# Graph attention on one core: GpSimd waits for a step's four gathers before it issues the next four

## The chip, the cores and the metric

The kernel runs on one core of a Trainium2 chip. The metric is the device time of one execution, in microseconds. The kernel before took 6796.57 us, the median of three runs (6765.51 to 6805.92).

## The reference, cut to what matters

The program has eight layers on a graph of 3125 nodes and 50000 edges, each node with 256 features. Layers 0, 2, 4 and 6 work on the graph, the others are mixtures of experts. The change lies in the third graph layer alone, which is attention over the edges, run twice (two inner layers of weights):

```python
def _ga_layer(h, src, dst, Wq, Wk, Wv, Wo, g, b):
    q = (h @ Wq).reshape(n, H, DK)          # 8 heads of 32
    k = (h @ Wk).reshape(n, H, DK)
    v = (h @ Wv).reshape(n, H, DV)
    e = jnp.sum(q[dst] * k[src], axis=-1) / np.sqrt(DK)
    m = jax.ops.segment_max(e, dst, num_segments=n)
    a = jnp.exp(e - m[dst])
    z = jax.ops.segment_sum(a, dst, num_segments=n)
    alpha = a / (z[dst] + 1e-09)
    msg = v[src] * alpha[:, :, None]
    agg = jax.ops.segment_sum(msg, dst, num_segments=n).reshape(n, H * DV)
    return _layer_norm(agg @ Wo + h, g, b)
```

For each edge the row of its source node is needed: its keys and its values, 2 times 256 floats. These rows lie side by side in a table in HBM, and a gather fetches them.

## The kernel before, in words

The edges are sorted by their destination and cut into 416 chunks of 128 edges (CHUNKS). A gather fetches the 128 rows of one chunk, 2 KB each, from the table `pairs` to the 128 partitions; it is an indirect DMA that GpSimd issues, with a column of `by_dst_idx` as its list of rows. Four chunks (GS) are a step, so an attention has S = 104 steps and 416 gathers, and the two of them have 832.

A step's rows go to one of ten slots (SLOTS): seven in the tile `held`, three more lent by the tile `xn`, whose content is parked in HBM meanwhile. Each slot has a semaphore of its own, `gathered[j]`, which rises by 16 with each gather that lands. GpSimd's part is the loop below. Before step i it waits until VectorE has done the messages of step i - 10 (`weighed`), whose slot it will fill.

```python
for i in range(S):
    if i == HELD:
        pool.wait_ge(parked, 16)
    if i >= SLOTS:
        pool.wait_ge(weighed, i - SLOTS + 1)
    for n in range(GS):
        k = GS * i + n
        nc.gpsimd.indirect_dma_start(rows(i)[:, n, :], None, K.pairs, ...).then_inc(gathered[i % SLOTS], 16)
```

The other engines run through loops of S + 9 steps written out in full, each with its own order. In VectorE's step i stand, in this order:

- `multiply(i - 2)`, line 1954: two products of queries (in PSUM) and keys (gathered). It is the one place that waits for `gathered`.
- in some steps `shift`, `lower` or `rescale`, lines 2004 to 2027, for the running maximum of the softmax. Every four steps (GW) make a wave of 128 rows of scores, and these parts stand once in a wave.
- `place(i + 1)`, line 1850: the one-hot matrices of the next step.
- `peaks_of_rows` once in a wave, lines 1981 to 1984.
- `score(i - 2)`, line 1963: the sums over the features of a head.
- `weigh(i - 8)`, line 1971: the values times their weights; it gives the slot back to GpSimd.
- `carry` once in a wave, lines 1992 to 2000.

So the gathers of step i may begin after VectorE's step i - 2, and their rows are wanted in its step i + 2.

TensorE makes the queries of the edges (line 2071) from transposed one-hots (line 2126), and sums the messages by node (line 2085). ScalarE copies the transposed one-hots out of PSUM (line 2184) and the sums of finished nodes to the result (lines 2159, 2161). SyncE only parks `xn` and fetches it back after the last step that uses the lent slots. There are other indirect DMAs in the kernel (lines 387, 1608, 1614), in other stages; no change touches them.

Of the kernel before, what the change touches and what calls it, by code (L numbers as in the profile page):

```python
# [57 lines left out]
GS = 4  # L58
# [1800 lines left out]
SLOTS = HELD + LENT  # L1859


def attention(nc, K, edges, G, q, acc):
# [6 lines left out]
    with stage(nc) as st:  # L1869
# [20 lines left out]
        gathered = [st.sem(f"gathered{j}") for j in range(SLOTS)]  # L1890
# [12 lines left out]
        def rows(i):  # L1903
            j = i % SLOTS
            return held[:, j, :, :] if j < HELD else lent[:, j - HELD, :, :]
# [5 lines left out]
        def load(engine, where, most):  # L1911
            _, values = nc.values_load_multi_w_load_instructions(
                where, [engine], min_val=0, max_val=most,
                skip_runtime_bounds_check_because="number_chunks writes tiles that there are and starts of banks of sums")
            return values

        with nc.Block() as block:

            @block.gpsimd
            def _(pool):  # L1920
                for i in range(S):
                    if i == HELD:
                        pool.wait_ge(parked, 16)
                    if i >= SLOTS:
                        pool.wait_ge(weighed, i - SLOTS + 1)
                    for n in range(GS):
                        k = GS * i + n
                        nc.gpsimd.indirect_dma_start(rows(i)[:, n, :], None, K.pairs,  # L1928
                                                     bass.IndirectOffsetOnAxis(ap=edges.idx[:, k:k + 1], axis=0))\
                            .then_inc(gathered[i % SLOTS], 16)  # L1930
# [780 lines left out]
```

## Time and profile before

| | |
|---|---|
| median of the runs | 6796.57 us |
| lowest and highest | 6765.51 and 6805.92 us |
| profiled execution: its own time | 6830.38 us |
| profiled execution: span from first to last instruction | 6828.6 us |
| GpSimd (POOL) busy | 2167.3 us, 32% of the span |
| first gather of the first attention, last start of a gather | 2976.6 us, 3732.2 us |
| first gather of the second attention, last start of a gather | 3947.7 us, 4723.4 us |

Every duration and point of time further down is of the profiled execution, which took 33.8 us more than the median of the runs. POOL is GpSimd, DVE is VectorE, ACT is ScalarE, PE is TensorE's matmuls. In an engine's timeline the columns are start, duration, engine, line, operation and tiles; in brackets stand the idle time before the instruction and what ended it. A gather's duration there is the time that GpSimd is busy with issuing it, not the time until its rows have landed.

### The profile page before, as it was taken

To read this page: it belongs to the slowest core of one execution; us is meant where nothing else is said; L and a number is where in the kernel's file an instruction comes from. 1 tells how busy PE (TensorE), PEld (TensorE's weight loads), DVE (VectorE), ACT (ScalarE), POOL (GpSimd) and SP (SyncE) were. 2 spreads that over 40 slices of the span, in tenths; PEclk is the share of its full clock that TensorE was granted. 3 is DMA by queue.
4 is the path that set the end of the run, shared out by engine and by line. 5 is a ranking of instruction groups with operands and counts; after the bars stand their busy time and mean duration, and the time that the engine had idled before them with its cause. 6 is when DMAs were issued, how large, how long until landed. Compare 5 with 4: busy or idle time off the path is not lost. (4 is left out here: it accounts for less than half of the span.)

```text
span 6828.6 us, 83598 instructions
## 1 busy us (share of the span) xinstructions
PE 4909.0 (72%) x21926; PEld 3369.3 (49%) x21975; DVE 2801.8 (41%) x6736; ACT 1757.8 (26%) x4567; POOL 2167.3 (32%) x2105
## 2 busy tenths in 40 slices
PE   2521649998794979567777657777679599999944
PEld 2410327745691458445555435555578544444443
DVE  4271459901324032447767456666332302020242
ACT  1220115400220012125555325555232200000020
POOL 3356220054345514236655055554004200000024
PEclk9999999999797978789889788888788799999966
DMA  0000003254464415445544154544115532424233
GB/s 15 1 1 1 1 26 135 99 187 135 134 196 139 145 56 184 152 134 149 150 134 133 55 156 133 142 138 123 55 44 180 178 138 74 177 73 174 77 89 113
DMA packets 345481, 755.43 MB, mean 111 GB/s; under 512 B 106057, under 2 KB 179380, under 8 KB 342006
## 3 DMA queue, kind: packets, MB, share of 16 engines
q1 hardware_dynamic: 185702, 435.52, 18.6%
q0 software_dynamic: 114208, 281.05, 14.6%
q10 hardware_dynamic: 45296, 35.56, 1.7%
q8 instruction: 129, 2.11, 0.1%
q14 instruction: 146, 1.20, 0.1%
HBM read 634.70 MB, written 117.24 MB: 110 GB/s over the span
## 5 line engine op out<-in xcount | busy, mean ns | idle before, releaser
L1178 PE MATMUL banks<-ring,xn 128*128 128x512 f32 (+1 forms) x3500 | 1349.0, 548 | 121.3 <-PEq L126 104.6
L1178 PEld LDWEIGHTS banks<-ring,xn 128*128 128x128 f32 x3500 | 627.9, 191 | 843.0 <-issue 826.0
L1928 POOL DMA_INDIRECT held<-pairs,by_dst_idx x592 | 644.5, 1089 | 829.4 <-POOLq L126 379.7
L2071 PE MATMUL banks<-agg,hotT 128*128 x1664 | 519.9, 442 | 226.3 <-ACT hotT L2184 119.0
L387 POOL DMA_INDIRECT dst_table<-nodes_pay,nodes_row x392 | 387.9, 990 | 777.1 <-DVEq L1152 404.7
L387 POOL DMA_INDIRECT bin_table<-bins_pay,bins_row x392 | 403.6, 1030 | 591.7 <-ACTq L795 205.3
L2071 PEld LDWEIGHTS banks<-agg,hotT 128*128 128x128 f32 x1664 | 328.7, 214 | 339.4 <-issue 291.6
L2159 ACT ACTIVATE x<-banks x832 | 323.5, 389 | 601.6 <-PE banks L2085 357.8
L1652 PE MATMUL banks<-second,hT 128*128 x1544 | 390.1, 392 | 41.0 <-ACT hT L1670 15.8
L1637 PE MATMUL banks<-xT,w1r 128*128 128x128 f32 x3088 | 402.5, 283 | 21.0 <-DVE xT L1690 8.7
L1670 ACT ACTIVATE hT<-banks,b1T 128x128 f32<-128x128 f32 x772 | 224.5, 368 | 721.6 <-PE banks L1637 528.9
L2085 PE MATMUL banks<-bins_pay,hot 128*128 128x264 f32 x832 | 290.3, 460 | 159.9 <-issue 110.8
L1637 PEld LDWEIGHTS banks<-xT,w1r 128*128 128x128 f32 x3088 | 381.6, 199 | 24.9 <-issue 18.1
L1070 PE MATMUL banks<-spans,lanes 128*128 128x256 f32 x1440 | 332.0, 387 | 77.6 <-DVE spans L1051 65.4
L1189 ACT ACTIVATE agg<-banks 128x512 f32<-128x512 f32 (+1 forms) x70 | 34.8, 549 | 1348.3 <-PE banks L1178 1348.3
L2509 DVE TENSOR_SCALAR yT<-banks,columns 128x512 f32<-128x512 f32 (+1 forms) x42 | 27.2, 689 | 839.5 <-PE banks L2490 839.5
L1698 DVE TENSOR_TENSOR bins_pay<-banks,bias 128x256 f32<-128x256 f32 x235 | 99.8, 425 | 646.8 <-PE banks L1652 537.8
L1556 POOL MEMSET second<- 64x8192 f32 x1 | 6.9, 6919 | 1126.5 <-POOLq L126 1126.5
L725 PE MATMUL banks<-places,loT 64*128 64x14 bf16 (+1 forms) x784 | 177.4, 226 | 241.8 <-issue 127.3
L2085 PE MATMUL banks<-nodes_pay,hot 128*128 128x264 f32 x832 | 279.7, 434 | 95.5 <-issue 69.9
L1614 POOL DMA_INDIRECT home_rows<-bins_pay,home x235 | 233.1, 992 | 360.8 <-DVE bins_pay L1698 343.8
L1070 PEld LDWEIGHTS banks<-spans,lanes 128*128 128x128 f32 x1440 | 266.5, 191 | 144.0 <-issue 111.2
(382 smaller groups left out, 8158.3 us busy)
## 6 DMA issues: line engine op xcount, KB each, us to landing
ring<-adjacency SPq DMA_DIRECT2D x145, 1280.0 KB
w1r<-in_L_ffn_W SPq DMA_DIRECT2D x114, 512.0 KB
adjacency<-strips SPq DMA_DIRECT2D x13, 3200.0 KB
w1r<-in_L_ffn_w SPq DMA_DIRECT2D x65, 512.0 KB
rows<-home_rows SPq DMA_DIRECT2D x35, 640.0 KB
ring<-adjacency SPq DMA_DIRECT2D x25, 640.0 KB
table<-xn SPq DMA_DIRECT2D x100, 128.0 KB
pairs<-ring SPq DMA_DIRECT2D x50, 256.0 KB
```

The lines of the kernel that those rows point to most:

```text
L387: self.nc.gpsimd.indirect_dma_start(self.table, bass.IndirectOffsetOnAxis(ap=self.row[:, c:c + 1], axis=0), self.pay[:, c * W:(c + 1) * W] ...
L725: nc.tensor.matmul(bank, loT[h * L:(h + 1) * L, c % 4, b * P:(b + 1) * P], places[h * L:(h + 1) * L, c * UB + b, :, :].rearrange("p d n -> ...
L1070: nc.tensor.matmul(K.banks[:, bass.ds((v % 16) * SPAN_S, SPAN_S)], lanes[:, j, q, :], spans[:, j, q, :], start=False, stop=True, skip_grou ...
L1178: last = nc.tensor.matmul(K.ps[2 * (g % 2) + o][:, 0:wd], x[:, t * D + o * P:t * D + (o + 1) * P], ring.buffer[:, n % R, 0:wd // cols, q * ...
L1614: nc.gpsimd.indirect_dma_start(K.home_rows, bass.IndirectOffsetOnAxis(ap=r.home[:, c:c + 1], axis=0), yr[:, c % R, :], None).then_inc(stor ...
L1637: last = nc.tensor.matmul(K.ps[2 + jj % 2][:, h * P:(h + 1) * P], w1r[:, jj, s, h * P:(h + 1) * P], xT[:, jj % 2, s * P:(s + 1) * P], star ...
L1652: last = nc.tensor.matmul(bank, hT[:, jj % 2, h * P:(h + 1) * P], ahead.second[:, bass.ds(e * (nh * D) + h * D, D)], start=(h == 0), stop= ...
L1670: last = nc.scalar.activation(hT[:, j % 2, h * P:(h + 1) * P], K.ps[2 + j % 2][:, h * P:(h + 1) * P], func, bias=b1T[:, bass.ds(e * nh + h ...
L1928: nc.gpsimd.indirect_dma_start(rows(i)[:, n, :], None, K.pairs, bass.IndirectOffsetOnAxis(ap=edges.idx[:, k:k + 1], axis=0))\
L2071: last = nc.tensor.matmul(queries(c, part)[:, n % 2 * D:(n % 2 + 1) * D], hotT[:, c % 2, n * P:(n + 1) * P], tile_of(q, at[n]), start=True ...
L2085: nc.tensor.matmul(K.banks[:, bass.ds(starts[n], W)], hot[:, g % HOTS, n, :], K.spare[g % MSGS][:, n * W:(n + 1) * W], start=False, stop=T ...
L2159: nc.scalar.activation(tile_of(acc, t, W), bank, ACT.Copy).then_inc(kept, 1)
```

## The change

One wait is added to GpSimd's loop. Before it issues the four gathers of step i, it waits until the four of step i - 1 have landed. Nothing is removed or moved, and the number of gathers, their order and their slots stay as they were.

```diff
                     if i >= SLOTS:
                         pool.wait_ge(weighed, i - SLOTS + 1)
+                    if i:
+                        pool.wait_ge(gathered[(i - 1) % SLOTS], 16 * GS * ((i - 1) // SLOTS + 1))
                     for n in range(GS):
                         k = GS * i + n
                         nc.gpsimd.indirect_dma_start(rows(i)[:, n, :], None, K.pairs,
```

## Rows read from the trace of the kernel before

**Rows 1.** The page: the span, and the gathers' group of instructions.

```profile
span 6828.6 us, 83598 instructions
...
L1928 POOL DMA_INDIRECT held<-pairs,by_dst_idx x592 | 644.5, 1089 | 829.4 <-POOLq L126 379.7
```

**Rows 2.** The two attentions in windows from VectorE's first product to its last.

```profile
core 0: us, PE busy (x) PEld busy (x) DVE busy (x) ACT busy (x) POOL busy (x), PEclk, DMA share, GB/s
...
2991.93:3746.20 754.27, 540.57 (x2198) 382.18 (x2196) 515.21 (x938) 381.62 (x1037) 438.06 (x410) 0.87 0.51 144
...
3963.12:4737.36 774.24, 545.51 (x2196) 383.99 (x2194) 515.06 (x939) 381.44 (x1037) 433.52 (x410) 0.86 0.50 140
```

**Rows 3.** Line 1928, both attentions: what ended GpSimd's idle time (us, times), and who waited.

```profile
L1928 POOL DMA_INDIRECT held<-pairs,by_dst_idx x592: 947/953/7122, 2976.6 to 4723.4; - x198
...
  DVE nodes_pay L1971: 289.5, 41
...
  DVE bins_pay L1971: 103.5, 27
...
  DVE held L1954: 19.2, 6
```

**Rows 4.** GpSimd's timeline, start of each attention: fourth gathers of a step, and the fortieth.

```profile
2988.10 0.95 POOL L1928 DMA_INDIRECT held<-pairs,by_dst_idx  x1 [0.30 <-issue]
...
2998.15 0.95 POOL L1928 DMA_INDIRECT held<-pairs,by_dst_idx  x1 [0.30 <-issue]
...
3033.63 0.96 POOL L1928 DMA_INDIRECT xn<-pairs,by_dst_idx  x1 [0.30 <-issue]
...
3959.20 0.95 POOL L1928 DMA_INDIRECT held<-pairs,by_dst_idx  x1 [0.30 <-issue]
```

**Rows 5.** VectorE's timeline: products that waited for those gathers, and the last ones.

```profile
2991.93 1.29 DVE L1954 TENSOR_TENSOR held<-banks,held 128x512 f32<-128x512 f32 x2 [5.64 <-DMA held<-pairs,by_dst_idx]
...
3001.82 1.29 DVE L1954 TENSOR_TENSOR held<-banks,held 128x512 f32<-128x512 f32 x2 [1.75 <-DMA held<-pairs,by_dst_idx]
...
3746.20 1.28 DVE L1954 TENSOR_TENSOR held<-banks,held 128x512 f32<-128x512 f32 x2
...
3963.12 1.29 DVE L1954 TENSOR_TENSOR held<-banks,held 128x512 f32<-128x512 f32 x2 [5.71 <-DMA held<-pairs,by_dst_idx]
...
4737.36 1.28 DVE L1954 TENSOR_TENSOR held<-banks,held 128x512 f32<-128x512 f32 x2
```

**Rows 6.** GpSimd's timeline: four gathers after a wait for VectorE's messages.

```profile
3221.44 0.95 POOL L1928 DMA_INDIRECT held<-pairs,by_dst_idx  x1 [3.19 <-DVE nodes_pay L1971]
3222.69 1.17 POOL L1928 DMA_INDIRECT held<-pairs,by_dst_idx  x1 [0.30 <-issue]
3224.17 1.96 POOL L1928 DMA_INDIRECT held<-pairs,by_dst_idx  x1 [0.30 <-issue]
3226.43 0.95 POOL L1928 DMA_INDIRECT held<-pairs,by_dst_idx  x1 [0.30 <-issue]
```

**Rows 7.** VectorE's timeline of the same stretch.

```profile
3219.96 1.22 DVE L1971 TENSOR_TENSOR nodes_pay<-held,weights 128x1024 f32<-128x1024 f32 x1
3221.09 1.28 DVE L1954 TENSOR_TENSOR held<-banks,held 128x512 f32<-128x512 f32 x2
...
3222.36 0.68 DVE L1850 TENSOR_TENSOR hot<-iota,by_dst_pay 128x512 f32<-128x512 f32 x1
...
3224.09 1.21 DVE L1971 TENSOR_TENSOR bins_pay<-held,weights 128x1024 f32<-128x1024 f32 x1
3225.22 1.28 DVE L1954 TENSOR_TENSOR held<-banks,held 128x512 f32<-128x512 f32 x2
```

**Rows 8.** Windows after the last gather of a burst has been issued (columns as in rows 2).

```profile
3385.46:3387.55 2.09, 2.09 (x13) 1.49 (x11) 0.82 (x4) 1.25 (x4) 0.00 (x0) 1.00 0.67 214
3387.75:3392.50 4.75, 2.20 (x8) 1.63 (x9) 4.68 (x9) 2.58 (x8) 0.63 (x1) 0.87 0.00 0
```

**Rows 9.** ScalarE's and GpSimd's timelines, around the end of the first forty gathers.

```profile
3032.68 0.60 ACT L2184 ACTIVATE hotT<-banks 128x512 f32<-128x512 f32 x1 [25.42 <-remote]
```

```profile
3056.24 0.95 POOL L1928 DMA_INDIRECT held<-pairs,by_dst_idx  x1 [21.65 <-DVE bins_pay L1971]
```

**Rows 10.** VectorE's timeline, two products one step apart.

```profile
3400.82 1.28 DVE L1954 TENSOR_TENSOR held<-banks,held 128x512 f32<-128x512 f32 x2
...
3412.98 1.27 DVE L1954 TENSOR_TENSOR xn<-banks,xn 128x512 f32<-128x512 f32 x2
```

## The prediction, made before the change was run

> **What bounds the kernel now.** I read the page first, for the size of the matter: 592 of the 832 gathers stand in one group there, 1089 ns each [rows 1]. Then windows over the two attentions: from the first product to the last they take 754.27 us and 774.24 us, and no engine fills them; TensorE is busy for 540.57 of the 754.27 us, VectorE for 515.21, GpSimd for 438.06, the DMA engines for half [rows 2]. An attention has 104 steps, so 103 intervals lie between its first and last product: 7.32 us and 7.52 us a step. Then the line of the gathers: GpSimd's idle time is ended 68 times by VectorE's line 1971, 393.0 us in all (289.5 + 103.5), while VectorE waited for gathered rows six times, 19.2 us [rows 3]. All six lie in the first steps. So the gathers run ahead and the computing engines set the pace, in a ring of dependences between TensorE, ScalarE and VectorE. The reader is to see that GpSimd has slack, about 190 us in each attention, and that the question is whether the added wait is larger.
>
> **The change: one wait, 103 times in each attention.** What it makes is a loop of GpSimd and the DMA engines alone: issue four, wait for the landing of the fourth, issue four. Behind the wait on GpSimd's queue stand only gathers; SyncE's and the other queues are not touched. Who waits for the gathers is VectorE's line 1954. The length of the loop is a sum of four terms.
>
> (1) From the first issue to the fourth: three intervals of 0.95 us issue and 0.30 us gap [rows 4], 1.256 us each, 3.77 us.
>
> (2) From the start of the fourth issue to the moment its rows can be used. The trace shows it where VectorE waited for it: the fourth gather began at 2988.10 and the product at 2991.93, 3.83 us; the twelfth at 2998.15 and the product at 3001.82, 3.67 us; in the second attention 3959.20 and 3963.12, 3.92 us [rows 4, 5]. I take 3.8 us. Those gathers had others right behind them, which the new loop won't have. The other end: after the last issue of a burst ended, at 3385.46, data flowed for 2.09 us more and then the DMA engines stood still [rows 8]; with 0.95 us of issue that is 3.0 us, and the semaphore can't come earlier. So 3.0 to 3.9.
>
> (3) GpSimd's start after a semaphore. After line 1971 ended at 3221.18 (3219.96 + 1.22), GpSimd began at 3221.44, 0.26 us later, and VectorE's product began with the same event or a little before [rows 6, 7]. In term 2 VectorE's start is already contained, so I add 0.2 us; the ends are 0.1 and 0.35.
>
> (4) Stretched issues. An issue takes 0.953 us at the median and 1.089 us in the mean [rows 1, 3]: 0.136 us by four, 0.54 us a step. The timelines show where it comes from. The third gather after 3221.44 began at 3224.17 and took 1.96 us, while VectorE's line 1971 ran from 3224.09 to 3225.30; the second began at 3222.69, inside line 1850 (3222.36 to 3223.04), and took 1.17 us [rows 6, 7]. Line 1954 does not do this. In this example the four span 4.99 us instead of 3.77. In the new loop GpSimd and VectorE are released by the same event, the landing, so they stand to each other as in these rows, in which both were released together: about 1.3 us in two of a wave's four steps (plain ones, with line 1971 some 3 us after the product), and 0.1 to 0.4 us in the two where the maximum's work delays line 1971. That mean would be 0.8 us. I take 0.7, between this and 0.54.
>
> The rule behind term 4 is in the Trainium skill, "SBUF — State Buffer", section "Who interferes with whom": a VectorE instruction with two SBUF inputs contends with a GpSimd instruction that reads SBUF, and the later one blocks. The trace agrees (line 1971 and line 1850 have two SBUF inputs, line 1954 has one in PSUM). The same section infers that such an instruction doesn't hinder the making of descriptors; the 1.96 us issue speaks against this for indirect gathers, which read their indices. By that inference term 4 would be nothing, and the loop 0.7 us shorter.
>
> The loop: 3.77 + 3.8 + 0.2 + 0.7 = 8.47 us a step.
>
> **What hides it.** The computing engines need 7.32 and 7.52 us a step in the mean, less than the loop. They do need more in single steps (12.2 us between two products, 3400.82 and 3412.98 [rows 10]), but the gathers of step i may begin four steps before they are wanted, and that lead carries such a step. So the loop sets the pace nearly everywhere. The first rows land as before, at 2991.9 and 3963.1. The last product then comes 103 times 8.47 = 872.4 us after the first: 118.2 us later than now in the first attention (872.4 - 754.27), 98.2 us in the second. The work after the last product is the same. Sum: +216 us.
>
> A second way to count it: each wait costs GpSimd 3.8 + 0.2 less the 0.95 us of issue and the 0.30 us gap that were there, 2.75 us, by 103 is 283 us. By 2 it is 566 us, of which 393 us of idle time [rows 3] can swallow at most that much: +173 us, and +206 with 0.16 us more stretch a step. The two agree.
>
> Profiled, 6830.4 + 216 = 7046 us; the profiled execution was 33.8 us above the median, so for the median 6796.6 + 216 = **7013 us**, 3.2% slower.
>
> **Something that speaks for the change.** During the first forty gathers, which run without a pause to 3033.63 [rows 4], ScalarE stood for 25.42 us before a copy at 3032.68, put down to nothing local, although TensorE's transposes had their last recorded end long before; when the burst was over this stopped. GpSimd then idled 21.65 us until 3056.24 [rows 9]. If a long burst holds back other engines, spacing the gathers removes that, and the computing engines alone could be quicker than 7.3 us. With a loop of 8.47 us it doesn't matter how much quicker: the gain is only in how the first ten steps run, and the sum from first to last product contains it. It would matter if the loop were shorter.
>
> **Rivals.**
> *The landing is quick enough, and nothing changes.* The loop would have to be 7.1 to 7.75 us (206 intervals times p, less 1528.5 us, within 68 us of zero; 68 us, 1%, is about what a measurement of this kernel can tell from no change). With term 2 at 3.0, term 3 at 0.1 and term 4 at 0.54 it is 7.41, so -2 us: 6795 us. For it: the drain of 2.09 us [rows 8]. Against it: three measured waits of 3.67 to 3.92 [rows 4, 5]. 12%.
> A sentence apart: by the Trainium skill, "DMA: Bandwidth & Descriptors", section "Anatomy of one DMA — SWDGE (gpsimd) path", a DMA takes 2.0 us plus its bytes by 436 GB/s, 2.6 us for 256 KB as an estimate from that page. Counted from the start of the issue this would give the same rival, with a loop of some 7.3 us; counted from its end it gives 3.55 us and the forecast. The rows above lie with the second.
>
> *Faster.* The burst is what holds TensorE's results back, in later bursts too, and the loop is short. Were it 6.9 us, the time would fall by 107 us, to 6690 us. It decides from a loop below 7.1 us, for which the landing has to come 2.5 us after the fourth issue begins, less than the 3.0 us at which data still flowed [rows 8]. 3%.
>
> *Slower than forecast: both bounds add up.* Two ways to the same price. The slow single steps outlast the lead, so that VectorE gives the slot back late and the loop starts late; or TensorE, which waits longer in each step, is granted less of its clock than the 0.87 of now [rows 2] and needs its 5.2 us a step (540.57 by 104) nearly twice. Either gives about 9.2 us a step: +367 us, 7164 us. For it: rows 10. Against it: 12.2 us is one step among four. 18%.
>
> *The wait does nothing.* It would have to be over when GpSimd comes to it. That holds where GpSimd idles longer than 2.75 us for line 1971 anyway; there are at most 68 such places [rows 3] for 206 waits, and they are in the second count above. No chance of its own.
>
> **How the numbers follow.** Forecast (loop 7.9 to 8.9 us) 67%, unchanged 12%, faster 3%, both bounds 18%. The range leaves out the faster case and most of the unchanged one, and takes in the upper one but for its tail: a loop of 7.65 us gives 6796.6 + 47 = 6844, of 9.2 us 7164; 6850 to 7165 us. Faster by over 1% 3%, within 1% 12%, slower by over 1% 85%.
>
> **What the new profile would show.** Right, if GpSimd's idle time before line 1928 is ended by the landing of gathers some 200 times with nearly 3 us each; if VectorE's line 1954 waits for the gathers in most steps; if groups of four gathers start about 8.5 us apart, with the third often 1.9 us long; if the two windows from first to last product are near 872 us. The burst of forty is gone, and ScalarE's 25 us wait with it. Wrong, if the landing comes 3 us after the fourth issue starts, or if VectorE still never waits for rows.

## The result, and the profile after

The changed kernel took 7101.47 us, the median of three runs (7095.71 to 7102.41), against 6796.57 us before: 1.0434 times as long, 95% interval 1.0399 to 1.0469. The profiled execution took 7095.71 us; against the profiled one of before that is 265 us more, between the medians it is 305 us. The profiled execution of before lay 34 us above its median, that of after 6 us below its own.

The page of the changed kernel, its span and the gathers' group (line 1930 is line 1928 of before):

```profile
span 7094.0 us, 83788 instructions
...
L1930 POOL DMA_INDIRECT held<-pairs,by_dst_idx x592 | 665.3, 1124 | 998.5 <-DMA held<-pairs,by_dst_idx 423.4
```

The two windows from VectorE's first product to its last, as in [rows 2]:

```profile
2987.98:3885.36 897.38, 593.95 (x2196) 416.98 (x2194) 515.60 (x938) 384.36 (x1042) 447.41 (x412) 0.84 0.44 121
4101.70:5004.23 902.53, 603.79 (x2194) 421.43 (x2194) 515.10 (x939) 383.72 (x1042) 452.03 (x412) 0.82 0.43 120
```

The reader is to see that the work in them is the same as before, VectorE's 515 us within half a microsecond, while the windows have grown by 143.1 us (897.38 - 754.27) and 128.3 us (902.53 - 774.24). That is 271.4 us, all of the 265.4 us between the spans and a little more. By 103 intervals the steps take 8.71 and 8.76 us, where they took 7.32 and 7.52.

Line 1930 of the changed kernel: what ended GpSimd's idle time, and who waited for gathers (compare [rows 3]):

```profile
  DMA held<-pairs,by_dst_idx: 489.5, 144
...
  DMA xn<-pairs,by_dst_idx: 203.2, 60
...
  DVE held L1956: 548.0, 148
...
  DVE xn L1956: 217.3, 60
```

GpSimd now waits for landings 204 times, 3.4 us each, and no longer for VectorE's messages at all. VectorE waits for gathered rows at each of its 208 pairs of products. Both stand still for the same event, which is what a loop of issue and landing looks like from its two sides.

GpSimd's timeline over one step and the start of the next:

```profile
3173.78 0.95 POOL L1930 DMA_INDIRECT held<-pairs,by_dst_idx  x1 [3.37 <-DMA held<-pairs,by_dst_idx]
3175.04 0.96 POOL L1930 DMA_INDIRECT held<-pairs,by_dst_idx  x1 [0.30 <-issue]
3176.30 1.86 POOL L1930 DMA_INDIRECT held<-pairs,by_dst_idx  x1 [0.30 <-issue]
3178.47 0.96 POOL L1930 DMA_INDIRECT held<-pairs,by_dst_idx  x1 [0.30 <-issue]
3182.81 0.95 POOL L1930 DMA_INDIRECT held<-pairs,by_dst_idx  x1 [3.39 <-DMA held<-pairs,by_dst_idx]
```

VectorE's timeline beside it:

```profile
3173.11 1.29 DVE L1956 TENSOR_TENSOR held<-banks,held 128x512 f32<-128x512 f32 x2 [1.93 <-DMA held<-pairs,by_dst_idx]
...
3176.12 1.22 DVE L1973 TENSOR_TENSOR bins_pay<-held,weights 128x1024 f32<-128x1024 f32 x1
3182.14 1.29 DVE L1956 TENSOR_TENSOR held<-banks,held 128x512 f32<-128x512 f32 x2 [4.80 <-DMA held<-pairs,by_dst_idx]
```

From these the terms can be read for one step. The fourth issue began at 3178.47 and the product that needs it at 3182.14: 3.67 us. GpSimd, released by the same landing, began at 3182.81: another 0.67 us. The four issues span 4.69 us, 0.92 more than 3.77, with the third stretched while line 1973 (1971 of before) ran beside it.

### The profile page after: what moved, and what is told of

It reads as the page before. It is cut to its first block and busy times, and to the rows that moved or that the text cites. A ratio compares the mean times of both kernels' runs of the same rounds, so it can differ in the third digit from the quotient of the medians.

```text
span 7094.0 us, 83788 instructions
## 1 busy us (share of the span) xinstructions
PE 5023.2 (71%) x21926; PEld 3443.5 (49%) x21975; DVE 2802.3 (40%) x6736; ACT 1761.6 (25%) x4567; POOL 2192.3 (31%) x2105
## 5 line engine op out<-in xcount | busy, mean ns | idle before, releaser
L1930 POOL DMA_INDIRECT held<-pairs,by_dst_idx x592 | 665.3, 1124 | 998.5 <-DMA held<-pairs,by_dst_idx 423.4
L2073 PE MATMUL banks<-agg,hotT 128*128 x1664 | 553.2, 463 | 254.9 <-DVE held L1956 151.2
L2087 PE MATMUL banks<-bins_pay,hot 128*128 128x264 f32 x832 | 349.2, 538 | 308.3 <-DVE banks L2029 256.4
L1956 DVE TENSOR_TENSOR held<-banks,held 128x512 f32<-128x512 f32 x296 | 190.8, 686 | 548.0 <-DMA held<-pairs,by_dst_idx 548.0
L2087 PEld LDWEIGHTS banks<-bins_pay,hot 128*128 128x128 f32 x832 | 205.8, 272 | 382.7 <-issue 351.4
```

The lines of the kernel that those rows point to most:

```text
L1956: V.tensor_tensor(keys, queries(c, hh)[:, 0:2 * D].rearrange("p (c d) -> p c d", d=D), keys, ALU.mult).then_inc(product if hh else halved, 1)
L2073: last = nc.tensor.matmul(queries(c, part)[:, n % 2 * D:(n % 2 + 1) * D], hotT[:, c % 2, n * P:(n + 1) * P], tile_of(q, at[n]), start=True ...
L2087: nc.tensor.matmul(K.banks[:, bass.ds(starts[n], W)], hot[:, g % HOTS, n, :], K.spare[g % MSGS][:, n * W:(n + 1) * W], start=False, stop=T ...
```

## The experiments

They ran in three groups, each on one chip, beside the kernel before on that chip. The kernel before took 6719 us on the chip of the first group, 6109 us on that of the second and 6112 us on that of the third, a third chip. Within a chip its runs differ by less than 1%. So ratios are compared within a group, and steps across groups. A trace of the kernel before exists for the chip of the result ("the first chip" below) and for that of the third group; for the first and second groups only its times are known. The changed kernel itself ran on the first chip and in the third group.

**Waiting for fewer of the four.** Three runs in which GpSimd waits for the first three, two or one gathers of the step before. For these the waited-for gathers have semaphores of their own, and VectorE waits for both:

```diff
+        EARLY = 3    # 2 in the second run, 1 in the third
+        early = [st.sem(f"early{j}") for j in range(SLOTS)]
...
-                        pool.wait_ge(gathered[(i - 1) % SLOTS], 16 * GS * ((i - 1) // SLOTS + 1))
+                        pool.wait_ge(early[(i - 1) % SLOTS], 16 * EARLY * ((i - 1) // SLOTS + 1))
...
-                            .then_inc(gathered[i % SLOTS], 16)
+                            .then_inc((early if n < EARLY else gathered)[i % SLOTS], 16)
```

> GpSimd waits only for the first three gathers of the step before (they have a semaphore of their own; VectorE waits for both). Theory, the loop of issue and landing sets the pace: the loop loses one issue interval of 1.26 us, from the 8.74 us of the changed kernel to about 7.4 us a step; the 2 times 103 intervals then take about as long as in the kernel before, 6800 us in all, within 40. Rival, the added wait costs something else than the loop (waits that add up with the computing engines' own slow steps): the steps stay near 8.2 us or more, 6960 us or more.

Measured: 6777.94 us, 1.0092 times the kernel before (1.0075 to 1.0109); 7.25 us a step. The step lost 1.5 us for one issue left out of the loop, where 1.26 us were expected, and the rival's 8.2 us or more did not come. GpSimd's idle time is ended by landings 177 times here, by VectorE's messages 28 times, so the loop still sets most steps, but not all. Windows from the first product to the last of the first attention, waiting for three:

```profile
2981.23:3728.10 746.87, 548.97 (x2196) 386.54 (x2194) 517.15 (x938) 381.30 (x1042) 439.53 (x411) 0.89 0.51 146
```

> GpSimd waits only for the first two gathers of the step before. The loop is about 6.2 us, shorter than the 7.3 to 7.5 us a step of the kernel before, so the loop can't slow it. Theory of the bursts (long runs of gathers without a pause hold TensorE's results back, and the loop allows at most four gathers in 6.2 us): the steps come down to 6.2 to 6.8 us, 150 to 250 us less than the kernel before, 6550 to 6650 us. Rival (the pace of the kernel before is that of its computing engines and has nothing to do with bursts): 6800 us, within 30.

Measured: 6649.29 us, 0.9907 (0.9882 to 0.9931): 0.9% faster than the kernel before on that chip, 70 us, about half of the 150 us that the theory of the bursts gave at least. The steps came to 6.56 and 6.63 us. Waiting for two, the same window:

```profile
2986.25:3662.29 676.04, 513.45 (x2198) 364.43 (x2196) 513.79 (x939) 380.02 (x1037) 445.79 (x410) 0.92 0.57 161
```

> GpSimd waits only for the first gather of the step before. The loop is then no longer than the four issues, about 5.0 us, so bursts are nearly what they were. Theory of the bursts: little or nothing is gained, 6750 to 6800 us. Rival: 6800 us as well; together with the run that waits for two it shows whether the pacing or the wait itself matters.

Measured: 6722.76 us, 1.0011 (0.9996 to 1.0025), 6.96 us a step. So the wait as such does nothing, and what helps on that chip is the pace of two, although GpSimd has to wait for a landing only 40 times with it, 30.7 us in all (29 times and 8.9 us when it waits for one).

The traces of these slower chips also say what the pace does to the late results of TensorE that the prediction describes under "Something that speaks for the change". They appear as waits of ScalarE and VectorE that are put down to nothing on the core ("remote"). Summed over the two attentions they come, on the chip of this group, to 268 us with a wait that never holds GpSimd up (the next run), 297 us waiting for one gather, 196 us waiting for two, and none at all waiting for three. On the first chip they come to 417 us in the kernel before and to none in the changed kernel. For ScalarE's copy of the transposes alone, the kernel before (line 2184) and the run that waits for one (line 2189) have:

```profile
  remote: 122.5, 36
```

```profile
  remote: 66.0, 13
```

So long bursts and late results go together on these chips. But where the pace is slow enough that none is left, the loop is itself about as long as the steps were with them, 7.25 us waiting for three.

**The wait without its content.** It stands where it stood, for gathers long landed:

```diff
-                    if i:
-                        pool.wait_ge(gathered[(i - 1) % SLOTS], 16 * GS * ((i - 1) // SLOTS + 1))
+                    if i >= 3:
+                        pool.wait_ge(gathered[(i - 3) % SLOTS], 16 * GS * ((i - 3) // SLOTS + 1))
```

> The wait stands where it stood, but for the step three before, whose gathers have landed by then. What is left is the instruction. Theory: as the kernel before, 6800 us within 30, since GpSimd has some 190 us of slack in each attention and the instruction costs at most 0.5 us a step. Rival, the wait as an instruction is what costs: 6900 us or more.

Measured: 6716.89 us, 1.0003 (0.9986 to 1.0021). Its line 1930 shows the idle time before gathers ended by VectorE's messages again and not by landings, as in [rows 3]:

```profile
  DVE nodes_pay L1973: 174.2, 33
  DVE bins_pay L1973: 109.8, 30
  DMA xn<-pairs,by_dst_idx: 0.3, 1
```

The instruction is free while GpSimd has slack; the cost of the change is the landing. One detail matters below. Here too two waits stand in front of the first gather of a step, and the one that comes true last is VectorE's. GpSimd and VectorE's line 1973:

```profile
3122.93 0.95 POOL L1930 DMA_INDIRECT held<-pairs,by_dst_idx  x1 [3.37 <-DVE bins_pay L1973]
```

```profile
3121.43 1.23 DVE L1973 TENSOR_TENSOR bins_pay<-held,weights 128x1024 f32<-128x1024 f32 x1 [4.74 <-ACT weights L2179]
```

GpSimd starts 0.27 us after the end of line 1973 (3121.43 + 1.23), and it does so all 63 times, exactly as in the kernel before with its single wait (68 times, 0.27 us).

**Only one wait in front of a gather.** The wait for VectorE's messages is moved one gather ahead:

```diff
-                    if i >= SLOTS:
-                        pool.wait_ge(weighed, i - SLOTS + 1)
...
                     for n in range(GS):
                         k = GS * i + n
+                        if n == GS - 1 and SLOTS <= i + 1 < S:
+                            pool.wait_ge(weighed, i + 1 - SLOTS + 1)
```

> The changed kernel, but the wait for VectorE's messages moves from the first gather of a step to the last gather of the step before, so that no gather has two waits in front of it. Theory, term 3 of the sum was too small (0.2 us) because the second wait becomes an instruction of its own, after which GpSimd starts 0.67 us behind VectorE's product instead of 0.17: the loop loses 0.5 us in some 93 steps of each attention, 8.74 to about 8.25 us, and the time against the kernel before falls from 1.043 to about 1.030. Rival, the start is slow for another reason (VectorE holding the port, the landing seen later by GpSimd): 8.7 us and 1.043 stay.

Measured: 8.22 and 8.25 us a step, as expected. 6604.63 us, 1.081 (1.0792 to 1.0828), not 1.030: the expected ratio went by the kernel before of the first chip, and on this chip that kernel is 10% faster. The changed kernel was not run on this chip. The nearest comparison is with the third group, where the kernel before takes the same time within 0.1%: the changed kernel has 1.0988 and 8.70 and 8.74 us a step there. GpSimd's timeline in this run:

```profile
2805.91 0.95 POOL L1930 DMA_INDIRECT held<-pairs,by_dst_idx  x1 [3.06 <-DMA held<-pairs,by_dst_idx]
...
2815.04 0.95 POOL L1930 DMA_INDIRECT held<-pairs,by_dst_idx  x1 [3.00 <-DMA held<-pairs,by_dst_idx]
```

And VectorE's:

```profile
2805.74 1.29 DVE L1956 TENSOR_TENSOR held<-banks,held 128x512 f32<-128x512 f32 x2 [1.74 <-DMA held<-pairs,by_dst_idx]
...
2814.88 1.29 DVE L1956 TENSOR_TENSOR held<-banks,held 128x512 f32<-128x512 f32 x2 [4.91 <-DMA held<-pairs,by_dst_idx]
```

GpSimd now begins 0.17 us after VectorE's product instead of 0.67, and the rival falls. The changed kernel's own trace shows the same thing within a few steps: up to step 9 of an attention only the new wait stands in front of the first gather (but for step 7, which waits for `parked` as well), from step 10 on both. The first gathers of steps 9 and 10 on GpSimd, and VectorE's products released by the same landings:

```profile
3053.29 0.95 POOL L1930 DMA_INDIRECT xn<-pairs,by_dst_idx  x1 [2.84 <-DMA xn<-pairs,by_dst_idx]
...
3062.11 0.95 POOL L1930 DMA_INDIRECT held<-pairs,by_dst_idx  x1 [3.13 <-DMA xn<-pairs,by_dst_idx]
```

```profile
3053.12 1.29 DVE L1956 TENSOR_TENSOR xn<-banks,xn 128x512 f32<-128x512 f32 x2 [4.77 <-DMA xn<-pairs,by_dst_idx]
...
3061.43 1.29 DVE L1956 TENSOR_TENSOR xn<-banks,xn 128x512 f32<-128x512 f32 x2 [2.37 <-DMA xn<-pairs,by_dst_idx]
```

0.17 us, then 0.68. (Step 7, at 3036.62, starts 0.70 us after its product.) The page of the changed kernel also counts 190 instructions more than that of the kernel before (83788 and 83598), and this run only 2 more. So a second wait beside the wait for the landing costs 0.5 us. A second wait as such does not: in the run for the step three before it stood there as well, and the start came at the usual 0.27 us. Which property decides, the order of the two or what the last one waits for, is open; the two waits in the other order were not run.

**VectorE's work, with and without its second SBUF input.** Both kernels leave out as much of VectorE's time (the windows show 438.08 and 435.49 us where it was 515); one takes it from the weighing, which reads two tiles in SBUF, the other from the sums, which read one.

```diff
-                    V.tensor_tensor(msg[g % MSGS][:, :, 0:DH]..., rows(g)[:, :, D:2 * D]..., ALU.mult)
+                    V.tensor_tensor(msg[g % MSGS][:, 0:HEADS, 0:DH]..., rows(g)[:, 0:1, D:2 * D]..., ALU.mult)
```

> The changed kernel with VectorE's weighing of the messages (two inputs in SBUF) done for one of the four chunks of a step; the other three quarters of this work are left out. Theory, term 4: this instruction stretches issues by up to 1 us, and the loop shortens by 0.4 to 0.7 us a step, from 8.74 to 8.0 to 8.3 us. If the loop didn't set the pace but VectorE's work did, it would shorten by the 0.9 us that are left out.

Measured: 8.41 and 8.45 us a step, 0.29 less than with all the work (8.70 and 8.74, third group). The direction is that of term 4, the size smaller than expected: issues take 404.86 by 412 = 0.983 us in the window below instead of 447.85 by 412 = 1.087, 0.42 us less a step, of which 0.29 arrive. The traces say where the rest stays. In the first attention the time from the first to the fourth issue's start falls from 4.23 to 3.94 us, all of the 0.29; the other 0.12 us are the fourth issue's own length, and from its start to the product it takes 3.84 us with the full work and 3.85 with a quarter.

```profile
2632.49:3499.21 866.72, 601.47 (x2198) 423.26 (x2196) 438.08 (x939) 383.70 (x1042) 404.86 (x412) 0.82 0.45 125
```

```diff
-                    V.tensor_reduce(scores[:, v % 2, at:at + GS * HEADS]..., rows(c)[:, :, 0:D]..., AX.X, ALU.add)
+                    V.tensor_reduce(scores[:, v % 2, at:at + HEADS]..., rows(c)[:, 0:1, 0:D]..., AX.X, ALU.add)
```

(the scores of the other chunks are set to zero once).

> The changed kernel with VectorE's sums over the features (one input in SBUF) done for one of the four chunks of a step; three quarters of this work are left out, as much VectorE time as in the run before. Theory, this instruction doesn't hold up an issue, and its absence only shifts the weighing by 0.9 us: the loop stays at 8.4 to 9.0 us. If VectorE's work set the pace, 7.8 us.

Measured: 8.67 and 8.68 us a step, 0.03 and 0.06 less than with all the work:

```profile
2631.42:3524.64 893.22, 600.32 (x2198) 422.85 (x2196) 435.49 (x938) 382.90 (x1042) 443.09 (x412) 0.83 0.44 122
```

So as much VectorE time as in the run before is taken away and next to nothing arrives. VectorE's work is behind the loop, and what matters of it is when it keeps GpSimd from issuing.

**Three gathers in the first ten steps, two afterwards.**

```diff
-                        pool.wait_ge(early[(i - 1) % SLOTS], 16 * EARLY * ((i - 1) // SLOTS + 1))
+                        pool.wait_ge(early[(i - 1) % SLOTS], 16 * (2 * ((i - 1) // SLOTS) + 3))
...
-                            .then_inc((early if n < EARLY else gathered)[i % SLOTS], 16)
+                            .then_inc((early if n < (3 if i < SLOTS else 2) else gathered)[i % SLOTS], 16)
```

> GpSimd waits for three gathers of the step before in the first ten steps and for two afterwards. Theory of the bursts: the stall of some 35 us in the steps 3 to 5, which the run that waits for two still has, goes, and each attention gains 10 to 15 us over it; 0.986 to 0.988 of the kernel before, against 0.991. Rival, the stall at the start comes from something else than the burst of forty gathers: 0.991.

Measured: 6169.88 us, 1.0095 (1.0079 to 1.0112), a loss. On this chip the kernel before was itself 10% faster than on the first, and this run's trace has no late results in the attentions, so it says nothing on the stall at the start.

**The same kernels on one more chip.** Nothing was edited.

> The kernel before once more, for its profile on this chip. On the chip of the second group of runs it took 6109 us, where the first trace was of an execution of 6830 us. Theory: the DMA engines and each single instruction take the same time on all chips, and what differs is TensorE's late results while gathers flow; so where the whole time is near 6110 us, the steps of the attention are near 5.9 us and no copy of ScalarE waits 10 us or more for a transpose that has ended; where it is near 6750 us, the steps are 6.9 to 7.5 us and such waits are there. Rival: the chip's instructions or its memory are faster throughout.

Measured: 6110.53 us. The windows of the kernel before on this chip:

```profile
2631.65:3231.34 599.69, 489.78 (x2198) 346.45 (x2196) 511.70 (x939) 377.53 (x1037) 465.94 (x410) 0.98 0.66 181
3447.14:4047.22 600.08, 487.76 (x2194) 344.78 (x2194) 512.60 (x938) 377.49 (x1037) 468.88 (x410) 0.99 0.65 181
```

5.82 and 5.83 us a step, where [rows 2] have 7.32 and 7.52. VectorE's and ScalarE's busy times are the same within about 1% and TensorE is granted 0.98 of its clock instead of 0.87. Line 2184, ScalarE's copy that stood for 25.42 us in [rows 9], waits for nothing here but transposes and the zeroing at the start:

```profile
  PE banks L2126: 65.5, 16
  DVE x L2034: 36.0, 2
```

And line 1928 shows another bound: GpSimd waits for VectorE's messages once, for 0.3 us, while VectorE waits for rows 30 times.

```profile
  DVE bins_pay L1971: 0.3, 1
...
  DVE held L1954: 41.0, 25
  DVE xn L1954: 7.3, 5
```

GpSimd's issues take 465.94 us of the 599.69 and the gaps of 0.30 us between 410 of them 123 more. Here the kernel before is bound by GpSimd's issuing. The two windows are shorter by 329 us than on the first chip, of 720 us between the whole executions; most of the rest lies ahead of the attentions, whose first gather starts at 2616.3 us here and at 2976.6 us there.

> The changed kernel beside the kernel before on one chip. Theory, its attention is set by GpSimd's loop, which is the same on every chip: 8.7 us a step here too. The ratio is then 1.043 to 1.055 where the kernel before takes 6700 to 6800 us, and about 1.098 where it takes 6110 us. Rival, the change costs 265 to 305 us everywhere: 1.045 to 1.05.

Measured: 6714.29 us, 1.0988 (1.097 to 1.1007), by the theory's figure of 1.098. The attentions of the changed kernel there:

```profile
2629.86:3526.29 896.43, 599.51 (x2194) 418.15 (x2194) 515.21 (x939) 383.01 (x1042) 447.85 (x412) 0.83 0.44 121
3744.62:4644.59 899.97, 600.65 (x2197) 418.94 (x2195) 514.96 (x939) 383.18 (x1042) 450.13 (x412) 0.83 0.43 121
```

896.43 and 899.97 us, against 897.38 and 902.53 us on the first chip: the loop is the same on both, while what it replaces is 600 us on the one and 754 to 774 us on the other. The two windows grow by 596.6 us here, nearly all of the 602.5 us between the medians (6714.29 - 6111.81).

> The wait for two gathers of the step before, again. Theory: a gain only where the kernel before has the late results: 0.988 to 0.993 of it on a chip on which it takes 6700 us or more, 1.00 to 1.01 on one on which it takes 6110 us, because the loop of 6.2 us is then slightly longer than the engines' own 5.9 us.

Measured: 6150.43 us, 1.0062 (1.0045 to 1.0079), as the theory had it; the steps take 6.02 and 6.04 us against the 5.82 and 5.83 us of the kernel before.

> Three gathers in the first ten steps, two afterwards, beside the run that waits for two throughout. Theory of the bursts: 0.985 to 0.990 where the kernel before takes 6700 us or more, 0.003 to 0.005 better than two throughout, and 1.0095 where it takes 6110 us, as measured. Rival: no better than two throughout on either chip.

Measured: 6174.58 us, 1.0101 (1.0084 to 1.0118), worse than two throughout. Whether it helps on a chip with the late results is open, as no run of it fell on one.

So no version beats the kernel before everywhere: waiting for two gains 0.9% on one chip and loses 0.6% on another.

## Why the prediction was right, point by point

**What bounds the kernel.** Right for the chip of the trace: GpSimd had slack, and the engines set the pace. On the chip of the third group it isn't so, which nothing in one trace could show; on that of the second the same 6109 us suggest it, without a trace of the kernel before.

**The loop.** The forecast was 8.47 us a step, measured 8.71 and 8.76. Over all steps of the two attentions in the changed kernel's trace, the parts are in the mean:

| | forecast | first attention | second attention |
|---|---|---|---|
| term 1, three intervals without a stretch | 3.77 | 3.77 | 3.77 |
| term 4, stretch between the first and the fourth start | 0.7 | 0.46 | 0.52 |
| term 2, fourth start to VectorE's product | 3.8 | 3.85 | 3.84 |
| term 3, product to GpSimd's next start | 0.2 | 0.63 | 0.64 |
| sum | 8.47 | 8.71 | 8.76 |

Term 3 was mis-sized most. It had been read where GpSimd waits for VectorE's message, and not where it waits for a landing with a second wait beside it; there the start comes 0.67 us after the product, and 0.17 us after it where the landing is the only wait, close to the forecast's 0.2. Term 4 was too large by 0.2 us. One reason lies in its lower end: the mean of 1.089 us in [rows 1] contains the first gathers of an attention, one of 7.12 us [rows 3], and the windows of [rows 2] give 1.07 and 1.06 us (438.06 by 410 and 433.52 by 410), 0.44 us a step instead of 0.54. The long issues did come where the forecast had them: in the wave from 3165 us the four issues span 3.78, 4.69, 4.95 and 3.79 us.

**What hides it.** Right: the engines' own work vanished behind the loop. Leaving out three quarters of the sums changed the step by 0.03 and 0.06 us, and TensorE, granted 0.84 and 0.82 of its clock instead of 0.87 and 0.86, stayed hidden with 5.8 us a step (593.95 by 103).

**The sum.** 216 us forecast; 271 us in the windows, 265 us between the profiled executions. Over 206 steps term 3 missed 89 us and term 2 another 9, and term 4, too large, gave back 44: the 55 us are what is left of errors that partly cancelled, so the nearness of the forecast owes something to luck. (118.2 us in the forecast should be 118.1, without effect.) The medians differ by 40 us more than the profiled executions, mostly the scatter of the kernel before.

**The rivals.** "Quick enough" would need a step of 7.75 us or less; it was excluded by the landing, which never came less than 3.5 us after the fourth start. "Faster" too, but its mechanism was partly real: on the first group's chip a pace of two waited-for gathers brought 0.9%. "Both bounds add up" didn't occur: 169 of the 206 steps take 8.2 to 9.5 us and the extremes are 7.5 and 11.5, where the kernel before has steps from 4 to 25 us. "The wait does nothing" fell with the 204 waits.

**The bursts.** The forecast left the late results aside, since a loop of 8.5 us makes them irrelevant. That held: in the changed kernel's attentions no wait is put down to them. On the slower chips they shrink with a pace of two and are gone with three or four (the sums above). That the bursts alone cause them can't be said: on the chip of the third group the same bursts run without them.

## What to carry to other kernels

A wait for a landing turns a queue of transfers into a loop, whose length is the issues plus the landing plus the wake-up; compare it with the time that a step takes now, and place the wait one or two transfers earlier if pacing is what is wanted. If the new bound is such a loop, its length carries over to other chips, but the gain or loss does not, because it is counted from what bound the kernel before. Look at the waits in front of an instruction on GpSimd: a second one beside the wait for a landing cost 0.5 us a step here, while one beside a wait for VectorE cost nothing.

## What the runs showed of the hardware that was not expected

- The same kernel took 6797, 6719, 6109 and 6112 us on four occasions, on at least three chips, each within 1%. In the attention the DMA-bound loop took the same 8.7 us on two of them, and single instructions too (line 1973 1.22 us, an issue 0.95 us). What differed in the attentions is that in the slower ones TensorE's results reach the other engines late while gathers flow: in the kernel before on the first chip, 36 of ScalarE's copies start 1.6 to 20.7 us after the last recorded end of a transpose, half of them more than 3.3 us; in the kernel before of the third group every copy that waited for a transpose starts 0.04 us after its end. Its cause stays open.
- A gather on GpSimd that waits for a landing with a second wait in front of it starts 0.67 us after VectorE's product released by the same landing, and 0.17 us after it when the landing is the only wait. Where VectorE's message is what comes last, it starts 0.27 us after it with one wait or with two.
- An indirect gather's issue, 0.95 us, waits for a VectorE instruction with two SBUF inputs that runs when it starts, up to 1.96 us in all; one with an input in PSUM, or with a single input, doesn't hold it. In the changed kernel's attentions 52 issues beside line 1850 and 136 beside line 1973 are stretched beyond 1.0 us, and all 188 end 0.82 to 0.84 us after the end of VectorE's instruction. Of the 206 issues that start during line 1956 (an input in PSUM) none takes more than 0.97 us, and of the 156 that start during line 1965 (one input) only one does, which lies beside line 1973 as well.
